# A root's widening set ahead of a projection, and a score mask written by eight products of a quarter column and half a row of the array

## The reference

```
for i in range(DEPTH):                                    # 6 layers
    x = attn_layer(shift_tokens(x), ...) + x
    x = ffn_layer(shift_tokens(x), ...) + x

attn_layer: q, k, v = x @ Wqkv                            # 16 heads of 64
            q, k = l2norm(q) * qs, l2norm(k) * ksc        # then rotary tables
            sim  = q @ k(own window of 32, and the one before) * 8
            sim  = where(mask, -max, sim); softmax; @ v; @ Wo
ffn_layer:  xn = (x - mean) / sqrt(var + 1e-5) * g + bln  # layer norm
            a, gate = split(xn @ W1 + b1);  a * gelu(gate) @ W2 + b2
```

## Time and profile before

| what | value |
| --- | --- |
| median of 3 runs | 1754.96 us (1753.17 to 1756.02) |
| the profiled execution's own time | 1753.95 us |
| its span, first to last instruction | 1752.2 us |
| mean granted TensorE clock | 0.966 of full |
| busy share of the span: PE, DVE, ACT, POOL | 91%, 83%, 64%, 60% |
| records: PE products, PE weight loads | 32061, 32157 |

### The profile page before, as it was taken

The page is one execution under the profiler, slowest core; times in us unless marked ns, Lnnn a source line. Parts: engine busy times, 40 slices in busy tenths (PEclk is TensorE's granted clock), DMA queues, the critical chain, the costliest instruction groups (busy, mean ns, idle before and its releaser), DMA issues.

```text
span 1752.2 us, 75843 instructions
## 1 busy us (share of the span) xinstructions
PE 1593.5 (91%) x32061; PEld 1277.3 (73%) x32157; DVE 1446.0 (83%) x3193; ACT 1115.9 (64%) x2014; POOL 1049.6 (60%) x1028
## 2 busy tenths in 40 slices
PE   5359999999999999999999999999999999999985
PEld 3237877778877778777778777777778777877863
DVE  8758988888988888889888878788889888888851
ACT  5226666667667667667667666666767666766652
POOL 2236766665666665666666657476576576575530
PEclk8569999999999999999999999999999999999997
DMA  2012111111111111111111111211111211011110
GB/s 85 30 32 60 37 39 36 57 42 47 36 44 36 57 42 48 31 48 37 57 43 47 32 41 34 60 36 51 40 36 40 60 36 47 27 44 52 29 40 13
DMA packets 41078, 74.97 MB, mean 43 GB/s; under 512 B 9472, under 2 KB 22568, under 8 KB 40744
## 3 DMA queue, kind: packets, MB, share of 16 engines
q1 hardware_dynamic: 40744, 70.12, 13.8%
HBM read 20.08 MB, written 2.10 MB: 13 GB/s over the span
## 4 chain that ended last, share of the span: by engine, by line
PE 74%; issue 8%; DVE 6%; ACT 4%; POOL 2%; ACTq 0%; DVEq 0%; POOLq 0%
PE bank L1258 8%; PE bank L1359 8%; PE bank L1292 8%; PE bank L1248 8%; PE wide L1330 7%; PE bank L1250 6%; PE bank L1249 6%; PE bank L1345 4%; PE bank L1310 4%; PE bank L1414 4%; PE bank L1282 2%; PE bank L1402 2%; PE bank L1404 2%; PE bank L1403 2%; ACT L1175 1%
## 5 line engine op out<-in xcount | busy, mean ns | idle before, releaser
L816 POOL TENSOR_TENSOR qk<-qk,rnorm 128x512 f32<-128x512 f32 x384 | 401.6, 1046 | 348.0 <-DVE rnorm L965 348.0
L808 POOL TENSOR_TENSOR qk<-qk,qk_sin 128x512 f32<-128x512 f32 x384 | 492.1, 1282 | 168.5 <-DVE qk_sin L928 168.4
L1107 ACT ACTIVATE squares<-bank 128x512 f32<-128x512 f32 x384 | 229.4, 598 | 154.3 <-DVE qk_sin L928 154.2
L938 DVE TENSOR_REDUCE norm<-squares 128x8 f32<-128x512 f32 x384 | 258.5, 678 | 30.9 <-ACT squares L1107 28.8
L1248 PE MATMUL bank<-w_hi,xs_hi 128*128 128x512 f32 x576 | 262.1, 455 | 13.4 <-ACT squares L1107 7.2
L921 DVE TENSOR_TENSOR qk<-bank,tables 128x512 f32<-128x512 f32 x384 | 261.9, 682 | 6.4 <-PE bank L1250 5.7
L928 DVE TENSOR_TENSOR qk_sin<-bank,tables 128x512 f32<-128x512 f32 x384 | 261.5, 681 | 0.7 <-POOL qk L808 0.6
L1250 PE MATMUL bank<-w_hi,xs_lo 128*128 128x512 f32 x576 | 230.1, 399 | 0.0
L1249 PE MATMUL bank<-w_lo,xs_hi 128*128 128x512 f32 x576 | 228.8, 397 | 0.0
L1258 PE MATMUL bank<-ident,qk 128*128 128x128 f32 x1536 | 225.4, 277 | 2.8 <-POOL qk L816 1.7
L1258 PEld LDWEIGHTS bank<-ident,qk 128*128 128x128 f32 x1536 | 180.1, 141 | 42.3 <-issue 3.1
(11 more groups left out here) (169 smaller groups left out, 2717.5 us busy)
## 6 DMA issues: line engine op xcount, KB each, us to landing
v<-v SPq DMA_DIRECT2D x96, 390.0 KB, 3.5
v<-v SPq DMA_DIRECT2D x72, 130.0 KB, 3.7
w_raw<-in_L_ffn_Wqkv SPq DMA_DIRECT2D x36, 256.0 KB, 3.8
w_o_s<-in_L_ffn_Wo SPq DMA_DIRECT2D x6, 512.0 KB, 6.2
w_raw<-in_L_ffn_W SPq DMA_DIRECT2D x6, 341.0 KB, 4.3
mix_x_nat<-in_L_attn_x SPq DMA_DIRECT2D x4, 256.0 KB, 3.4
x_res_scratch<-mix_x_res SPq DMA_DIRECT2D x4, 256.0 KB, 2.4
w_raw<-x_res_scratch SPq DMA_DIRECT2D x4, 256.0 KB, 4.2
```

The costliest lines, as they stand in the source:

```text
L808: pool.tensor_tensor(qk[:, g % 2, c, :], qk[:, g % 2, c, :], qk_sin[:, (QK_CHUNKS * g + c) % SINES, :], ALU.add).then_inc(added[c], 1)
L816: pool.tensor_tensor(view, view, rnorm[:, g % 2, c * HPC:(c + 1) * HPC].unsqueeze(2) .to_broadcast([P, HPC, DH]), ALU.mult).then_inc(norme ...
L938: dve.tensor_reduce(norm2[:, c * HPC:(c + 1) * HPC], squares[:, c % 2, :].rearrange("p (h d) -> p h d", d=DH), AX.X, ALU.add).then_inc(sum ...
```

## The change

In steps with t = 0 the widening stands right behind the second weighing, ahead of the projection Q1, instead of behind it. And the mask of each of the two banks is written by four products, each with 64 rows (one half of the mask's rows) by 32 columns of the array, eight in all, in place of two products on the whole array. The two halves of the rows go to the two banks, as in the scores. The stationary operand of each is the 64x32 piece of the identity that picks the first 32 rows of that half, and the moving operand is that half's 512 columns of the mask.

```diff
-                for r in range(2):
-                    pe.matmul(bank[4 + r][:], ident_bf[:], mask_bf[:, min(g % NBLK, 1), :], start=True, stop=True)
+                for h in range(4):
+                    for r in range(2):
+                        row = slice(DH * r, DH * (r + 1))
+                        pe.matmul(bank[4 + r][WINDOW * h:WINDOW * (h + 1), :], ident_bf[row, DH * r:DH * r + WINDOW],
+                                  mask_bf[row, min(g % NBLK, 1), :], start=True, stop=True)
...
                 weigh(step - 3, 1)
-                project(step, Q1)
                 if t == 0:
                     widen_rstd(item - 2)
+                project(step, Q1)
                 turn_o(step - 3, 0)
```

## The result

The changed kernel takes 1745.12 us in the median of five runs (1736.45 to 1748.96), the one before 1756.02 beside it (1753.17 to 1773.24): a ratio of 0.9943 [0.9921, 0.9966]. That is 10 us off by the ratio, faster by more than the 0.2% bound, where 17.6 were forecast: 1745.12 us lies inside the range (1722 to 1753), 7.7 us above the named 1737.4 and just above the 1730 to 1744 of the case called likeliest. The profiled execution took 1745.12 us, with a span of 1743.3 and a mean granted clock of 0.963.

What follows compares the result with a forecast made beforehand. TensorE, busy 91% of the span, was taken to bound the kernel. Mask 11.5 plus widening 6.1 gave 17.6 us off 1753.95, so 1736.4; with the median 1.0 us higher, 1737.4 us was named, range 1722 to 1753.

Steps and rivals of the forecast that it cites:

- the case called likeliest: Whole kernel: the mask and the earlier widening together take 17.6 us off, 1737.4 us, own range 1730 to 1744; chance 0.46.
- The mask: Eight mask products ahead of the scores: 0.22 us a step over 96 steps, 21.1 us, net 11.5 us after longer gaps.
- the best bound: Mask to first score takes 0.32 us, a gain of 0.22 us a step; turning's start to first score 0.75 us.
- the rival in which they share something: Mask products: no more than 4.9 array parts work at a time, 0.08 us gained a step, 1746.2 us; chance 0.17.
- the slower one: Mask products: column parts of a row half go one after another, 0.44 us more a step, 1791 us; chance 0.08.
- The widening: Steps with t = 0: widening ahead of Q1 starts the scaling 0.54 us sooner, 17 times, 9.2 us; 6.1 us kept.
- the third that I let be lost: Of the earlier widening's 9.2 us, a third goes to interrupted scores (33 gaps in 96 steps), leaving 6.1 us.
- the 0.28 us that I left standing: Steps with t = 0: of the mask's 0.82 us idle for the scaling, 0.54 us goes and 0.28 us stays.
- What the scores' interruptions take back: Late instructions inside the scores: 33 gaps grow, giving back 7.3 and 2.3 us; gaps go from 32 to about 42 us.
- Nothing given back: Rival on the "issue" gaps in the scores: they neither grow nor multiply, 30.3 us off, 1724.7 us; chance 0.16.
- Another engine takes over: Rival on VectorE's row maximum: it starts no sooner in most steps, some 2 us gained, 1753 us; chance 0.13.
- the second rival: Mask products: the array parts share something, 8.8 us off in all, 1746.2 us; chance 0.17.

## Why the prediction was right, and where it was short

**The mask.** Right: 0.75 us from turning to first score, the best bound. The parts work at once (the eight products of the step at 833.47 start within 0.03 us); the rival in which they share something is out (0.89 was its sign), and so is the slower one (1.41). The Trainium skill ("TensorE: Matmul & The Clock Gate", Part 3, measured speedup against the span model) is borne out for parts of 512 columns: the first score 0.22 us behind the first of eight products. Its sentence that weight loads overlap running products only on other rows is not: four of the eight use the same 64 rows.

**The widening.** The mechanism was right in each piece (0.54 us, five waits for the root, the mask 0.25 us behind the scaling), and alone it measured 8.3 us where 6.1 were named. Its interval (5.4 to 10.9) holds both 6.1 and the 9.2 with nothing lost; but the scores' gaps in that run did not grow (26.4 us against 32.1), so the third that I let be lost has no support. The mask's wait for the scaling fell to 1.9 us, not towards 10: of the 0.28 us that I left standing 0.10 is now the switch, and what is left between the turning and the mask (0.09 us between their records) is too short for the view of waits to list.

**What the scores' interruptions take back** is the step that failed, by its size. The mechanism named was the right one, instructions that arrive late, and the number for the scores came out nearly as forecast (42.6 for "about 42"). But I priced it as 33 gaps in fixed places that grow by 0.22 and 0.07 us each, and only among scores. The runs show borders every 256 instructions that slide along the program, so that other gaps open: 50 in place of 36, in projections and the turning too. They grew by 15.1 us as the view counts them and by 18.0 from start to start, where 9.6 (and 3.1 for the widening) were forecast; some 22 us were taken back in place of 12.7. The mask alone kept 4.9 us of 21.1 (0.7 to 9.1 by its interval) where 11.5 were forecast. Some 3 us of what was taken back stay open. That 42.6 met "about 42" was in part luck: the number was made of 33 growing gaps, and it came from 44.

**The rivals.** Nothing given back: refuted by the gaps. Another engine takes over: VectorE still waits 74.4 us for the scores, and TensorE got no new wait for squares or normalised chunks. The time fell close to the second rival's 1746.2 us by chance: the parts share nothing, and it was the late instructions that took more.

## What to carry to other kernels

Where a trace shows idle stretches without a cause inside a train of small products, number the engine's instructions and look up the landings of the instruction queue: if the gaps stand at one residue and end behind a landing, the train is limited by how fast instructions arrive, and much of the time saved in it is given back. There count instructions before columns: sixteen products that cost the array no more than eight lost some 19 us, and a reordering that only removes a wait (8.3 us) did no worse than a faster product (4.9 us, with intervals that overlap). The place of the borders is worth 12.5 us by itself, 0.7%, so a small difference between two variants of such a kernel may be theirs and not the edit's.

## What the runs showed of the hardware

- TensorE's instructions came in 16.4 KB transfers, one for each 256 by count, with a border at 195 or 196 modulo 256 in every kernel here. The first instruction behind a border followed the landing of its transfer by 1.0 to 1.6 us in 505 of 506 gaps. In the changed kernel most borders whose 256 instructions had taken under 3.0 us stalled (46 of 55), and 3 of 13 between 3.0 and 3.5.
- A transfer could begin late: 6.86 us behind the border before, in place of 1.17, at the gap of 4.46 us behind a stretch with a DMA share of 0.85.
- The lower of TensorE's two clock levels came behind some long gaps and not behind others: the granted clock was 0.60 of full in the two microseconds around the end of the gap of 4.46 us, and stayed at 1.00 behind the 2.97 us that ended at 326.21 in the changed kernel.
- A fulfilled wait instruction cost TensorE 59 ns in the loop and 110 ns ahead of it; 59 is more than five times the 11 ns of a score's record with its weight load.
- Going from the whole array to its parts took 0.10 us, ahead of the mask as it had ahead of the scores.
